# A Haar block with attention: one turn for sums and maxima, half of y_lo on GpSimd, bands spread, and another tail

## The reference

```python
ll, lh, hl, hh = haar_dwt(x)                      # 2x2 cells of x
fused = relu(bn(conv1x1(concat(ll, lh, hl, hh), fusion_w, fusion_b)))    # 1024 -> 256
sp_in = concat(mean over channels(fused), max over channels(fused))
spatial = sigmoid(conv7x7(sp_in)) * fused
ch_map = sigmoid(mlp(mean over pixels(spatial)) + mlp(max over pixels(spatial)))
projected = relu(bn(conv1x1(ch_map * spatial, proj_w, proj_b)))          # 256 -> 1024
out = haar_idwt(projected) + x
```

## Time and profile before

| | us |
|---|---|
| median of 3 runs | 2391.2 (2390.98 to 2392.24) |
| the profiled execution | 2397.32 |
| its span, first to last instruction | 2395.4 |
| busy in the span: PE, DVE, ACT, POOL | 2305.2, 2134.5, 1089.8, 483.3 |
| PE waiting for VectorE's sd (L868) | 22.6 in 16 waits |

### The profile page before, as it was taken

One profiled execution on the slowest core, in us unless ns is written; L12 is line 12 of the kernel. 1 busy time (PEld: TensorE's weight loads), 2 busy tenths in 40 slices (PEclk: granted clock), 3 DMA queues, 4 the chain that ended last, 5 costly groups with the idle time before them and its releaser, 6 DMA issues. The chain is left out here.

```text
span 2395.4 us, 30247 instructions
## 1 busy us (share of the span) xinstructions
PE 2305.2 (96%) x11109; PEld 2041.8 (85%) x11109; DVE 2134.5 (89%) x2773; ACT 1089.8 (45%) x1443; POOL 483.3 (20%) x467
## 2 busy tenths in 40 slices
PE   7999999999999999999999999999999999998797
PEld 6787889888898988989898888989889898886686
DVE  7877888899888998899988999889988899889798
ACT  4445534454344544455344553445434454435332
POOL 0010111111111111111111111111111111141799
PEclk9999999999999999999999999999999999999899
DMA  5455699999999999999999999999999999989898
GB/s 186 166 180 193 193 289 278 295 299 280 286 281 282 294 273 279 294 285 297 289 283 282 301 274 292 291 274 298 276 287 291 285 301 283 281 258 281 311 342 319
DMA packets 112616, 660.54 MB, mean 276 GB/s; under 512 B 17682, under 2 KB 18772, under 8 KB 112212
## 3 DMA queue, kind: packets, MB, share of 16 engines
q1 hardware_dynamic: 85108, 480.68, 52.0%
q0 software_dynamic: 27360, 177.94, 39.8%
HBM read 448.24 MB, written 210.33 MB: 275 GB/s over the span
## 5 line engine op out<-in xcount | busy, mean ns | idle before, releaser
L542 PE MATMUL pp<-y_hi,wp_hi 128*128 128x480 f32 (+1 forms) x1792 | 672.1, 375 | 42.4 <-DVE sd L868 22.6
L542 PE MATMUL pp<-y_lo,wp_hi 128*128 128x480 f32 (+1 forms) x1792 | 667.9, 373 | 0.0
L542 PE MATMUL pp<-y_hi,wp_lo 128*128 128x480 f32 (+1 forms) x1792 | 666.4, 372 | 0.0
L633 ACT ACTIVATE x_hi<-xin 128x1920 fp32r<-128x1920 f32 (+1 forms) x224 | 420.2, 1876 | 522.1 <-PE pfs L570 463.5
L570 PE MATMUL pfs<-x_hi,wf_hi 128*128 128x480 f32 (+1 forms) x1648 | 614.2, 373 | 7.5 <-DVE x_lo L781 7.0
L570 PE MATMUL pfs<-x_lo,wf_hi 128*128 128x480 f32 (+1 forms) x1648 | 612.0, 371 | 0.0
L570 PE MATMUL pfs<-x_hi,wf_lo 128*128 128x480 f32 (+1 forms) x1648 | 611.9, 371 | 0.0
L781 DVE TENSOR_TENSOR x_lo<-xin,x_hi 128x1920 fp32r<-128x1920 f32 (+1 forms) x224 | 461.4, 2060 | 133.7 <-ACT x_hi L633 133.7
L666 ACT ACTIVATE relu<-pp,t 128x480 f32<-128x480 f32 (+1 forms) x448 | 286.8, 640 | 374.3 <-PE pp L542 371.0
L457 POOL DMA_DIRECT2D xre<-in_x_dram x190 | 166.9, 879 | 1423.9 <-DVE xre L885 1423.9
L542 PEld LDWEIGHTS pp<-y_hi,wp_hi 128*128 128x128 f32 x1792 | 339.6, 190 | 92.2 <-DVE sd L868 28.7
(11 more groups left out here) (104 smaller groups left out, 1486.7 us busy)
## 6 DMA issues: line engine op xcount, KB each, us to landing
xin<-in_x_dram SPq DMA_DIRECT2D x160, 960.0 KB, 8.2
out_dram<-xre SPq DMA_DIRECT2D x160, 960.0 KB, 6.4
xre<-in_x_dram POOLq DMA_DIRECT2D x136, 960.0 KB, 10.2
xin<-in_x_dram SPq DMA_DIRECT2D x64, 800.0 KB, 7.4
out_dram<-xre SPq DMA_DIRECT2D x64, 800.0 KB, 5.5
xre<-in_x_dram POOLq DMA_DIRECT2D x54, 800.0 KB, 9.9
xre<-in_x_dram SPq DMA_DIRECT2D x24, 960.0 KB, 7.1
sigb<-sig_scratch SPq DMA_DIRECT2D x28, 400.0 KB, 7.5
```

The source lines that it names most:

```text
L542: mm = pe.matmul(pp[j][:, 0:n_px], w[:, kt, cols], y[:, s.pc, kt, 0:n_px], start=(kt == 0 and m == 0), stop=(kt == CT - 1 and m == 2))
L633: nc.scalar.activation(halves(x_hi, i, k), pairs(i, k), ACT.Copy).then_inc(xhi_ready[i], 1)
```

## The change

Five things:
1. One turn. The sums (GpSimd) and maxima (VectorE) of a tile go into one tile `stats` (in xre's buffer 3, 960 wide). VectorE takes the maximum one slot later, turns both at once and reduces twice. x_lower(k+1,1) of the slots 2 to 19 moves up to stand behind x_lower(k+1,0).
2. Half 1 of y_lo is made by GpSimd for every tile, from y_full, which ScalarE writes; GpSimd does so behind x_lower(k+1,1).
3. The 98 bands are spread: ten in a six-row slot, two in a five-row slot, slots 1 to 13.
4. Tile 97's x is added by DMA as well (kc - 91 from 2 to 6); buffer 3 now comes fourth in the tail's round and not first.
5. The very last half of x is added by VectorE, in two pieces, each stored at once.

```diff
         def adding(kc, i):
-            return kc + LAG < NT or kc + LAG - NT in GATED
+            return kc + LAG < NT or 2 <= kc + LAG - NT < LAST
...
-        tail_homes = [3] + home[-3:]
+        tail_homes = home[-3:] + [3]
...
         # gpsimd, body
+                if s.c_next and not s.next_is_first and s.a:
+                    if s.load_next:
+                        gp.wait_ge(xlo_ready[1], s.k + 2)
+                    lower(s.kn)
...
         # scalar, upper
-                if pooled(kc):
...
+                need(act, lo_pool, kc)
+                nc.scalar.activation(y_full[:, 0:n_px], fused[:, 1, ring(kc)], ACT.Copy,
+                                     scale=ch[:, 1:2]).then_inc(y_ready, 1)
...
         # vector
+            def bands(s):
+                due = [2 if px_of(k) < PXM else 10 for k in range(TILES)]
+                for at in range(sum(due[1:s.k]), min(sum(due[1:s.k + 1]), KS * NK)) if s.k < TILES else ():
...
+            def turn(s):
+                dve.wait_ge(f_ready, CT * s.k)
+                need(dve, stats_turned, s.k - 1)
+                nc.vector.tensor_tensor(stats[:, PXM:PXM + n], fused[:, 0, here], fused[:, 1, here], ALU.max
                                         ).then_inc(mx_ready, 1)
+                dve.wait_ge(sm_ready, s.k)
+                dve.wait_ge(mx_ready, s.k)
...
+                nc.vector.transpose(to[:, both_maps], stats[:, both_maps]).then_inc(stats_turned, 1)
+                for m, (result, op, ready) in enumerate(((blocksum, ALU.add, blocksum_ready),
+                                                         (blockmax, ALU.max, blockmax_ready))):
+                    nc.vector.tensor_reduce(result[:, block:block + blocks],
...
+                                            AX.X, op).then_inc(ready, 1)
...
         # vector, body
                 if s.load_next:
                     x_lower(s.k + 1, 0)
+                if s.load_next and other(s.k) != other(s.k + 1):
+                    x_lower(s.k + 1, 1)
                 if ahead and not s.a:
                     lower(s.kc)
-                elif s.c and not ahead:
+                if s.c:
                     butterflies(s, 0)
                     if s.phase == 0:
-                        turn_sums(s)
+                        turn(s)
                     if s.phase == LAST - 1:
                         pool_chunks(s)
                     cells(s, 0)
-                if s.c_next and not s.next_is_first and not ahead:
+                if s.c_next and not s.next_is_first:
                     lower(s.kn)
...
                 if s.turn and not (s.phase == 0 and s.c):
-                    turn_sums(s)
+                    turn(s)
                 if s.phase in GATED:
                     gate(s, GATED[s.phase][0])
-                if s.load_next and other(s.k) != other(s.k + 1):
-                    x_lower(s.k + 1, 1)
-                if s.a:
-                    channel_max(s)
                 if s.load_next and other(s.k) == other(s.k + 1):
                     x_lower(s.k + 1, 1)
-                if s.a:
-                    turn(s)
...
         # vector, after the last slot
+            for n in range(2):
+                x = xre[:, home[g], rows]
+                nc.vector.tensor_tensor(x, x, cell[:, g % 2, rows], ALU.add).then_inc(last_summed, 1)
```

More of the change, by code:

```diff
@@ L111, in haar_block @@
         sd = sb("sd", [P, 2, 2 * PXM])
-        sm = sb("sm", [P, PXM])
+        y_full = sb("y_full", [P, PXM])
         sigb = sb("sigb", [P, CPX])
@@ L311, in uses @@
             return sum(home[n] == home[g] and adding(*divmod(n, 2)) == by_dma for n in range(g + 1))
[L313 to L319, removed]
         def wait_lower(eng, kc):
-            eng.wait_ge(lo_ready, lowers(kc))
-            if pooled(kc):
-                eng.wait_ge(lo_pool, kc + LAG - NT)
+            eng.wait_ge(lo_ready, kc + 1)
+            eng.wait_ge(lo_pool, kc + 1)
         block = ctx.enter_context(nc.Block())
@@ L424, in _ @@
                 body(s)
-            store(NT - 1, 1)
+            half_px = 2 * px_of(NT - 1)
+            for n in range(2):
+                rows = slice(n * half_px, (n + 1) * half_px)
+                sp.wait_ge(last_summed, n + 1)
+                sp.dma_start(dram(out_v, NT - 1, 1)[:, rows], xre[:, home[-1], rows]).then_inc(stored[home[-1]], 16)
             for p in range(RING):
-                sp.wait_ge(stored[p], 16 * home.count(p))
+                sp.wait_ge(stored[p], 16 * (home.count(p) + (p == home[-1])))
         @block.gpsimd
@@ L462, in lower @@
                 n_px = px_of(kc)
[L463 removed]
+                gp.wait_ge(y_ready, kc + 1)
                 gp.wait_ge(hi_ready, CT * (kc + 1))
[L465 removed]
+                nc.gpsimd.tensor_tensor(y_lo[:, kc % 2, 1, 0:n_px], y_full[:, 0:n_px],
                                         y_hi[:, kc % 2, 1, 0:n_px].bitcast(F32), ALU.subtract).then_inc(lo_pool, 1)
@@ L478, in body @@
             def body(s):
-                if s.phase == LAST and pooled(s.kc):
+                if s.phase == LAST:
                     lower(s.kc)
@@ L487, in body @@
                     channel_sum(s)
-                if s.c_next and not s.next_is_first and pooled(s.kn) and not s.a:
+                if s.c_next and not s.next_is_first and not s.a:
                     lower(s.kn)
@@ L826, in _ @@
             dve.wait_ge(bias_ready, 3)
[L828 to L832, removed]
+            def bands(s):
+                due = [2 if px_of(k) < PXM else 10 for k in range(TILES)]
+                for at in range(sum(due[1:s.k]), min(sum(due[1:s.k + 1]), KS * NK)) if s.k < TILES else ():
+                    dy, j = divmod(at, NK)
+                    tap = taps[:, (j // KS * KS + dy) * KS + j % KS:][:, 0:1]
                     eye = eye_pad[:, dy:dy + H2]
@@ L850, in butterflies @@
                 n_px = px_of(s.kc)
[L851 to L854, removed]
+                if s.turn and i == 1:
                     dve.wait_ge(blocksum_ready, s.k)
+                    dve.wait_ge(blockmax_ready, s.k)
                 if not s.a:
@@ L905, in lower @@
                 n_px = px_of(kc)
[L906 to L918, removed]
-                                        ).then_inc(mx_ready, 1)
@@ L921, in turn @@
[L921 to L932, removed]
@@ L934, in turn_sums @@
-            def turn_sums(s):
-                block, px, n = span_of(s.k - 1)
-                blocks = -(-n // GROUP)
+                dve.wait_ge(hi_ready, CT * kc + 1)
+                nc.vector.scalar_tensor_tensor(y_lo[:, kc % 2, 0, 0:n_px], fused[:, 0, ring(kc)], ch[:, 0:1],
+                                               y_hi[:, kc % 2, 0, 0:n_px].bitcast(F32),
+                                               ALU.mult, ALU.subtract).then_inc(lo_ready, 1)
+            def turn(s):
+                block, px, n = span_of(s.k - 1)
+                here = ring_px((s.k - 1) // TILES, px, n)
+                blocks = -(-n // GROUP)
+                dve.wait_ge(f_ready, CT * s.k)
+                need(dve, stats_turned, s.k - 1)
+                nc.vector.tensor_tensor(stats[:, PXM:PXM + n], fused[:, 0, here], fused[:, 1, here], ALU.max
+                                        ).then_inc(mx_ready, 1)
@@ L1009, in body @@
                     cells(s, 1)
-                if 1 <= s.k <= KS:
-                    bands(s.k - 1)
+                bands(s)
                 if s.phase in GATED:
@@ L1023, in _ @@
                 body(s)
+            g = 2 * NT - 1
+            dve.wait_ge(xre_landed[home[g]], 16 * uses(g, False))
+            dve.wait_ge(cell_ready, 2 * (g + 1))
+            for n in range(2):
+                rows = slice(n * 2 * px_of(NT - 1), (n + 1) * 2 * px_of(NT - 1))
+                x = xre[:, home[g], rows]
+                nc.vector.tensor_tensor(x, x, cell[:, g % 2, rows], ALU.add).then_inc(last_summed, 1)
 _INS = ["x"] + ["L0_conv_" + n for n in (
```

51 lines of the change are left out of this document (19 added, 32 removed).

## The result

The changed kernel takes 2396.7 us (median of 20 runs), the kernel before 2391.8 (20 runs). The ratio is 1.0021, 95% interval [1.0013, 1.0029]: some 5 us slower, where I had forecast 3 us faster. The profiled executions say the opposite: 2394.07 against 2397.32, which is my forecast difference to a quarter of a microsecond. So two things are to be explained: the traces, and why other executions disagree with them.

What follows compares the result with a forecast made beforehand. TensorE was taken as the bound. Early +13.7, steady -13.1, tail -2.9, with about 0.7 us for shorter convolve waits, gave -3 us; carried from profile 2397.32 to median 2391.2: 2388.2 us, own range 2382 to 2395, wider range 2373 to 2401.

Steps and rivals of the forecast that it cites:

- slots 1 to 13: Early: new order makes VectorE end F + 11.6 (F: end of a slot's products) against 10.5 wanted; -1.4 us (-4 to +2).
- slots 14 and 15: Early: slot 14's transposes wait for the later turn, F + 7.1 against F + 2.2 before; +4.9 us.
- ring, slots 16 to 20: Early: a chain from gate through means, x_hi, x_lower and turn back to gate, 14.8 us a slot; +10.2 us (0 to +14).
- slot 21: First slot behind the early part: start near 272 instead of 258.59 forecast; no loss of its own.
- steady: Slots 21 to 111: VectorE gains 0.85 a slot, six phase-6 stops of 1.9 us vanish (-16.5), y_lo waits +3.4; -13 us.
- tail: Slots 112 to 132: homes, tile 97 by DMA and last half together; -2.9 us.
- The carry-over from the profile to the median: Whole kernel: the median, 6.1 us below the profiled time, was assumed to keep that difference after the change.
- Rival 2: Phase 5 of six images: GpSimd's y_lo late before project at 1390.53; 2405 us, half of that 2398; chance 0.14.
- Rival 3: Phase 6: stops remain because of sd, gain 0 there, early loss in force; 2402 us; chance 0.07.
- Homes: Tail: residual halves' new buffers wait for stores, maps' store queues behind that load, convolve moves; +6.3 us (0 to 9).
- Tile 97: Tail: with x added by DMA, TensorE's 11.5 us stop shrinks to 5 us; -6.5 us (-8 to -2).
- Last half: End of tail: VectorE adds in 2 x 0.9 us and the store goes in two; -2.7 us (-3.5 to -1).

Runs made afterwards that it cites:

- e1: The kernel before, unchanged, timed and profiled a second time (chip A): 2392.4 us, ratio 1.0001, profiled 2393.05.
- e2: The changed kernel, unchanged, timed and profiled a second time (chip A): 2401.8 us, ratio 1.0037, profiled 2400.34.
- e9: Changed kernel with SP issuing the load of x(k+2,1) ahead of the gate's second load in gated slots (chip C): 2396.6 us, ratio 1.0020.
- e5: e3's kernel with both halves of y_lo made by VectorE again, except the tail's tiles (chip B): 2378.0 us, ratio 0.9933.
- e4: Changed kernel with the last image's maps stored ahead of one residual load on SP: 2400.3 us, ratio 1.0031.
- e8: e3's kernel; in slot 112 VectorE's turn goes ahead of the butterflies, GpSimd's sum ahead of its issue of an addition: 2373.3 us, ratio 0.9911.
- e11: e3's kernel; in slot 112 SP stores the maps ahead of all, their load behind one store: 2368.6 us, ratio 0.9904.
- e12: e11's kernel plus e8's turn ahead of the butterflies in slot 112: 2366.8 us, ratio 0.9893.
- e3: Changed kernel with x_lower(k+1,1) of slots 2 to 19 back behind the turn and the first gate (chip A): 2367.3 us, ratio 0.9897.
- e10: e3's kernel run a second time, unchanged (chip C): 2370.1 us, ratio 0.9909.
- e7: e3's kernel with bands as before, 14 in each of slots 1 to 7 (chip B): 2371.9 us, ratio 0.9913.

## Why the prediction was wrong

The two second profiles, e1 and e2, were taken in one session on one chip, and each lies within 1.5 us of its kernel's median there. Their difference is +7.3 us. By the prediction's own terms (us; slots by their starts):

```
term                     forecast   e1 to e2   first pair
slots 1 to 13               -1.4       -1.7       -0.8
slots 14 and 15             +4.9       +6.1       +4.8
ring, slots 16 to 20       +10.2      +14.2      +13.3
slot 21                      0         +4.2       +2.3
steady, slots 22 to 111    -13.8      -12.4      -16.0
tail                        -2.9       -3.1       -6.9
sum                         -3.0       +7.3       -3.1
```

(First pair, slots 14 and 15: 203.93 - 171.82 = 32.1 after, 199.84 - 172.57 = 27.3 before; the others in the same way. The tail is what is left to the end of the span.)

- **The step that failed is the sum of the early part: its term for the ring, +10.2, was too small, and slot 21 behind the ring had no term at all.** The mechanism was right in its links: the order of x_lower, the chain over four engines, transposes 7.3 us behind F (I said 7.1). Its size was not, in two places. SP's queue adds a wait for x in three slots of the ring, together 3.5 us in the first profile of after and 4.3 in e2, which I had only at the high end: with that wait moved (e9) slots 16 to 20 take 68.3 us, against the 68.9 that I had summed; with it 72.1, and 73.0 in e2. And slot 21, the first behind the ring, pays for slow products behind the last stop: 2.3 to 4.2 us where I had 0, though I had counted just that, 1.65 us each, for the steady stops. Slow products behind the stop for the transposes make slots 14 and 15 of e2 longer too, by 1.2 us over the forecast. Ring, slot 21 and these two are 9.4 of the 10.3 us by which e1 to e2 misses the forecast; 1.4 lie in the steady part, and the rest is -0.5.
- **The carry-over from the profile to the median failed too**, and hid the first. The profiled execution of before held 3.3 us in its steady part that e1's doesn't. After varies by the length of its slow patches and by the tail's transfers: one execution 2394.1, another 2400.3. So the first pair flattered the change: steady -16.0 and tail -6.9 covered the early loss, and that its sum of -3.1 meets the forecast of -3.0 is luck. That the profile was 6.1 us above the median was a sign of it.
- Steady: right. The phase-6 stops vanish, 0.42 us behind LAST against 0.5, the transpose of 960 elements 1.18 us (mean of 80) against 1.2. Rival 2's wait, GpSimd's y_lo late in phase 5, is there, but costs 0.2 us an image; I had said "0 (to 1 us each)". Rival 3 didn't happen. e5 shows that the turn without GpSimd's y_lo leaves 1.28 us of the stop.
- Tail: the parts hold by their mechanism, less by their size. Homes moved convolve by 5.2 us in the first pair, but by 2.2 from e1 to e2 (6.3 forecast); e4, e8, e11 and e12 show that it is SP's queue and the DMA behind it. Tile 97: the stop fell by 7.5 in the first pair and by 6.4 from e1 to e2, and alone the edit is worth 6 us (6.5 forecast). Last half: from the start of the last cells to the end 10.0 us before, 8.6 and 8.2 after: -1.5 and -1.8, not -2.7; in e3, e10 and e4 it is 7.5, so -2.5. VectorE's additions took 1.9 us (1.8 forecast); what follows them grew from 3.9 to 4.4. In neither pair do these parts add up to the tail's term (-3.7 against -6.9, -6.0 against -3.1); what makes up the rest I didn't follow.
- What I didn't price alone: the bands and the turn were worth 7.1 us in slots 1 to 13 (e3, e7), and the new order cost 6.4 of it. The sum of -1.4 was near what came (-0.8 and -1.7), for a reason that concealed the choice. (The terms written for F + 11.6 add up to 11.45.) Asking of each edit alone what it does early would have shown that one of them should be left out.
- The Trainium skill's rule from "SBUF — State Buffer" ("Who interferes with whom"), that a VectorE instruction with two SBUF inputs contends with a GpSimd instruction that reads SBUF, agrees with this trace at a meeting place that I hadn't listed: in slot 111 the maximum starts 0.4 us ahead of GpSimd's y_lo, ends 0.4 us behind it and takes 2.41 us, against a mean of 0.67 us over all 112 (GpSimd, then VectorE):

```profile
2120.65 1.55 POOL L462 TENSOR_TENSOR y_lo<-y_full,y_hi 128x480 fp32r<-128x480 f32 x1
```

```profile
2120.23 2.41 DVE L913 TENSOR_TENSOR xre<-fused 128x400 f32<-128x400 f32 x1
```

In slot 112 it takes 1.40. That is 0.8 of the 2.7 us by which TensorE's idle time ahead of the last transposes grew (2.66 to 5.34 us).

## What to carry to other kernels

Price every edit of a bundle by itself before netting them: here one order that cost 29 us in the trace and 34 in the medians of one chip hid edits that together gain 22 to 25. A long stop of TensorE costs its length and then, where nothing hides it, products at half clock (2.3 to 4.2 us here), and that part varies from run to run, so it belongs in the term and in the range. Take a second profile of a kernel before a sum of a few us is carried over to its median: one execution held 3.3 us that the next didn't.

## What the runs showed of the hardware

- The length of a stop alone doesn't decide on the clock behind it. In e3 stops of up to 2.8 us in slots 14 to 20 left the granted clock at 1.00; in e10, the same kernel, the stop of 2.31 us was followed by a clock of 0.50 and 1.5 us of slow products (e3: 2.32 us, none). At one place in slot 19 the changed kernel's stop was 3.02 us with the clock at 1.00 behind it, and 2.37 us with 0.50 behind it in e2. In the kernel before the same stop of 1.92 us in phase 6 was followed by slow products in three images of six, and not the same three in the next profile.
- The more was queued on the DMA just before it, the longer one small transfer took. The maps' load of 50 KB, issued 0.5 us behind a residual load of 960 KB and 1.4 us behind another (e4), let convolve start 10.2 us later; issued 1.6 us behind one (before) 6.8 us later; issued 4 us behind the nearest one (after) 4.9 us later.
